# First attention: the sixth tile of each head transposed ahead of the eighth scores, the seventh right behind them

## What is computed

```python
h = _layernorm(x, axis=-1) * (1 + ca) + sa
x = x + ga * _L0_attn_ref(h, L0_attn_Wqkv, L0_attn_Wo)

# _L0_attn_ref: H = 16 heads, KV = 4 key heads, D = 128, S = 1024
xq, xk = rope(xq), rope(xk)
scores = jnp.einsum('bhsd,bhtd->bhst', q, k) * D ** (-0.5)
mask = jnp.triu(jnp.full((S, S), MASK_NEG, dtype=scores.dtype), 1)
probs = jax.nn.softmax(scores + mask[None, None], axis=-1)
att = jnp.einsum('bhst,bhtd->bshd', probs, v).reshape(B, S, H * D)
return att @ Wo
```

## Time and profile before

| | us |
|---|---|
| runs (three) | 751.27, 753.32, 753.81; median 753.32 |
| the profiled execution's own time | 751.87 |
| its span | 750.1 |
| PE busy (share of the span) | 705.2 (94%) |
| DVE busy | 550.5 (73%) |
| ACT busy | 442.1 (59%) |
| POOL busy | 386.4 (52%) |
| first attention, its 128 slots | about 38 to 434 of the span |

### The profile page before, as it was taken

How to read it: one execution, slowest core, us unless ns; L and a number is a source line. 1 busy time by engine, 2 the same in 40 slices (tenths; PEclk the granted TensorE clock), 3 DMA queues, 4 the chain that set the end, 5 groups by cost and what they waited for, 6 DMA issues and landing times. The chain is left out here.

```text
span 750.1 us, 12256 instructions
## 1 busy us (share of the span) xinstructions
PE 705.2 (94%) x4315; PEld 607.7 (81%) x4315; DVE 550.5 (73%) x1233; ACT 442.1 (59%) x921; POOL 386.4 (52%) x421
## 2 busy tenths in 40 slices
PE   8969989999999999999998889999989999899997
PEld 5858878888888888888887779998867787677787
DVE  4567686768776777687676868999788887566666
ACT  3757656666676756666665544235488767545432
POOL 3876556545863477534662322412498445116773
PEclk9999999999999999999999999999999999999999
DMA  7000001000000000004001024000100000000001
GB/s 259 15 8 8 8 22 56 9 8 15 11 20 8 15 14 10 14 8 172 20 8 50 1 59 112 1 1 1 56 2 1 1 1 1 0 3 1 1 1 58
DMA packets 19131, 19.85 MB, mean 26 GB/s; under 512 B 2174, under 2 KB 17022, under 8 KB 19070
## 3 DMA queue, kind: packets, MB, share of 16 engines
q1 hardware_dynamic: 17950, 18.40, 7.7%
q10 hardware_dynamic: 1120, 0.66, 0.3%
HBM read 18.01 MB, written 1.05 MB: 25 GB/s over the span
## 5 line engine op out<-in xcount | busy, mean ns | idle before, releaser
L909 POOL TENSOR_TENSOR at_swapped<-at_swapped,at_sin 128x512 f32<-128x512 f32 x40 | 52.1, 1303 | 130.2 <-ACT at_swapped L588 130.2
L610 ACT ACTIVATE at_probs<-at_probs,at_negmax 128x128 f32<-128x128 f32 (+7 forms) x128 | 99.6, 778 | 31.8 <-DVE at_negmax L710 29.9
L710 DVE CUSTOM_DVE_ANT_0 at_probs<-at_scores,causal 128x128 f32<-128x128 f32 (+7 forms) x128 | 96.0, 750 | 17.4 <-PE at_scores L60 16.3
L501 PE MATMUL at_turn<-ident_sb,at_probs 128*128 128x128 f32 x576 | 85.0, 274 | 11.3 <-DVE at_full_T_lo L726 9.1
L501 PEld LDWEIGHTS at_turn<-ident_sb,at_probs 128*128 128x128 f32 x576 | 66.5, 140 | 19.8 <-issue 11.4
L603 ACT ACTIVATE at_edge_T_hi<-at_turn 128x128 fp32r<-128x128 f32 (+3 forms) x128 | 55.5, 434 | 33.4 <-PE at_turn L501 33.0
L58 PE MATMUL at_scores<-at_kT_hi,room 128*128 128x512 f32 (+1 forms) x192 | 66.3, 345 | 3.4 <-DVE at_negmax L710 3.4
L603 ACT ACTIVATE at_full_T_hi<-at_turn 128x512 fp32r<-128x512 f32 x64 | 38.2, 597 | 49.8 <-PE at_turn L501 47.6
L59 PE MATMUL at_scores<-at_kT_lo,room 128*128 128x512 f32 (+1 forms) x192 | 66.5, 347 | 0.0
L60 PE MATMUL at_scores<-at_kT_hi,room 128*128 128x512 f32 (+1 forms) x192 | 66.5, 346 | 0.0
L726 DVE TENSOR_TENSOR at_edge_T_lo<-at_turn,at_edge_T_hi 128x128 fp32r<-128x128 f32 (+3 forms) x128 | 61.3, 479 | 1.3 <-ACT at_edge_T_hi L603 0.8
(11 more groups left out here) (445 smaller groups left out, 2294.9 us busy)
## 6 DMA issues: line engine op xcount, KB each, us to landing
at_wq_in<-L_attn_Wqkv SPq DMA_DIRECT2D x16, 128.0 KB, 2.2
at_wo_in<-L_attn_Wo SPq DMA_DIRECT2D x16, 128.0 KB, 2.0
staging<-L_ffn_routed_w SPq DMA_DIRECT2D x7, 256.0 KB, 4.5
wmod<-L_wmod SPq DMA_DIRECT2D x2, 768.0 KB, 4.3
at_wmod<-L_wmod SPq DMA_DIRECT2D x1, 1024.0 KB, 9.0
staging<-L_ffn_w_gate SPq DMA_DIRECT2D x1, 1024.0 KB, 6.2
staging<-L_ffn_w_up SPq DMA_DIRECT2D x1, 1024.0 KB, 8.3
staging<-L_ffn_w_down SPq DMA_DIRECT2D x1, 1024.0 KB, 10.7
```

What stands on the lines that cost most here:

```text
L501: mm = pe.transpose(p_turn[t % 2][:, b - b0, :], probs[:, s % 4, b * P:(b + 1) * P], m.ident[:, :])
L610: act.activation(row, row, ACT.Exp, scale=-1.0, bias=negmax[:, unit % 4:unit % 4 + 1], accum_out=rowsum[:, unit // NT % 2, i:i + 1])\
L710: dve.tensor_tensor_reduce(out=probs[:, s % 4, 0:width], in0=p_scores[s % 2][:, 0:width], in1=m.causal[:, S - width:], scale=-1.0, scalar= ...
L909: turning = pool.tensor_tensor(swapped[:, r % 2, :], swapped[:, r % 2, :], sin[:, cols], ALU.mult)
```

## The change

In slot 7 of every head, PE transposes tile 5 ahead of the scores of tile 7 and tile 6 right behind them. In slot 0 no tile is transposed any more. ACT writes the high half of tile 6 ahead of the exponentials of tile 7. DVE writes the low half of tile 5 ahead of the maximum of tile 7 and the low half of tile 6 behind it, both ahead of the add of the output projection. The same instructions are issued, 3349 rows of PE, 980 of DVE and 681 of ACT in both; only the order is another. GpSimd and the DMA queues keep theirs.

```diff
@@ PE, slot @@
+                    if i == NT - 1:
+                        turn(unit - 2)
                     scores(g, h, i)
                     if unit < 4:
                         value_job(4 + unit)
-                    if unit >= 2:
+                    if i == NT - 1:
+                        turn(unit - 1)
+                    elif unit >= 2 and i:
                         turn(unit - 2)
@@ PE, behind the slots @@
-                turn(KV0 * UNITS - 2)
@@ ACT, slot @@
-                    if unit >= 2:
+                    if unit >= 2 and i:
                         probs_hi(unit - 2)
+                    if i == NT - 1:
+                        probs_hi(unit - 1)
@@ ACT, behind the slots @@
-                probs_hi(KV0 * UNITS - 2)
@@ DVE, slot @@
+                    if i == NT - 1:
+                        probs_lo(unit - 2)
                     maximum(unit)
                     if i == 2 and head:
                         inverse_sums(head - 1)
-                    if unit >= 2:
+                    if i == NT - 1:
+                        probs_lo(unit - 1)
+                    elif unit >= 2 and i:
                         probs_lo(unit - 2)
@@ DVE, behind the slots @@
-                probs_lo(KV0 * UNITS - 2)
```

## The result

| | before | changed |
|---|---|---|
| median of the runs (17 each, us) | 752.78 | 754.85 |
| lowest and highest | 750.29 to 754.03 | 753.27 to 756.69 |
| ratio, 95% interval | | 1.0029 (1.0019 to 1.0040) |
| profiled execution: time, span | 751.87, 750.1 | 755.24, 753.4 |

The changed kernel takes 1.4 to 3.0 us more. The forecast was 754.6 with 1.3 us more by its sum. The time lies in the range, and in the upper half of the likeliest case's own (753.4 to 755.9). That the two times differ by 0.25 only is in part luck: the forecast started from a median of three runs, 753.32, which lies 0.54 above the one of 17, and its sum of 1.3 was 0.8 short of the 2.07 measured.

A forecast was written before the change was run, and what follows sets the result against it. TensorE is busy nearly throughout, so only its waits can give: 9.1 us in 17 places for DVE's low half. Terms 1.00 + 0.38 + 1.25 - 1.98 - 0.2 - 0.1 + 0.93 = +1.3 us give 754.6, range 750.4 to 757.0.

The forecast's parts named there:

- Direction, and no measurable gain: Whole kernel: +1.3 us by the sum, most likely no measurable change, since under 0.3% can hardly be told from none.
- estimate of 744.8: Whole kernel: counting all gaps aimed at as gain, 9.1 us less 0.55, gives 744.8; 3 in 100.
- PE takes tile 6 early, gains 0.21: Ordinary head end, tile 6's transposes: PE stalls 0.32 instead of some 0.53, gaining about 0.21 up to here.
- DVE 0.93 later, 0.69 of cover, 0.25 left: Ordinary head end: short maximum 0.93 later, ACT's slack covers 0.69, query projection copies and PE 0.24 to 0.25 later.
- Key ends lose the same, through the add of slot 5: Ends of heads 2, 5, 6, 9, 10, before a key projection: 0.25 lost each through a late add, +1.25 together.
- Third end, +0.38: Third head's end: DVE did not idle 0.14 there, so 1.07 of delay against 0.69 of cover, +0.38.
- Between groups -0.66 each: Three ends between groups: the 0.98 stall at tile 7 goes, 0.32 at tile 6 comes; -0.66 each, -1.98 together.
- First, 15th, last: Head ends: first -0.2, 15th -0.1, last +0.93 because tile 6's low half stands ahead of the second add.
- What the profile was to show: Changed profile: tile 6 wait about 0.15, none at tile 7 between groups, 0.6 or more ahead of `attend`.
- Rival 1: Ordinary and key ends: slack 0.93 or more, so nine ends gain 0.21 each; faster, 750.1; 20 in 100.
- rival 2: Slower, 756.6: between groups PE waits for ACT, price 1.98; or slack 0.15 smaller, price 1.5; 20 in 100.
- Rival 3: Whole kernel: the order hides itself, PE's waits move and no term survives; 753.3; 15 in 100.

The follow-up runs named there:

- e3: Changed kernel, but DVE writes the low half of tile 6 behind the short maximum again; 751.11 us, ratio 0.9976 to before.
- e5: Changed kernel, last end as before, tile 6's low half early on DVE only at ends 1, 4, 8, 12, 15; 747.88 us, ratio 0.9931 to before.
- e9: Changed kernel with two unused matmuls filling PE's wait in the third head, ahead of slot 5's output projection; 754.86 us, ratio 1.0028 to before.
- e2: Changed kernel with the last head's end as before; 753.45 us, ratio 1.0013 to before.
- e1: Kernel before with the change only at the ends of heads 1, 4, 8, 12 and 15; 749.42 us, ratio 0.9960 to before.
- e8: Kernel before with only tile 5 moved ahead of slot 7's scores, tile 6 left in slot 0; 756.22 us, ratio 1.0045 to before.
- e6: e5 with five DVE gate steps moved from the third head into the fourth; 747.02 us, ratio 0.9916 to before.
- e7: Kernel before with only the five DVE gate steps moved from the third head into the fourth; 750.38 us, ratio 0.9970 to before.
- e4: Changed kernel with five DVE gate steps moved from the third head into the fourth; 753.57 us, ratio 1.0007 to before.

## Why the prediction was right, and where it was short

- **Direction, and no measurable gain: right.** Closing nearly all of the 9.1 us gave no time back; the kernel is 0.29% slower, clear of noise and under the 0.3% that the prediction called hard to tell from none. The rule of the Trainium skill (Perfetto Trace Analysis, Optimization Strategy) with its estimate of 744.8 did not hold for this edit as it stood. What decided here is that the producer made earlier pushed other work of its own engine back (5.42 in place of 4.44 for the short maximum).
- **PE takes tile 6 early, gains 0.21: right.** In e3 and e5, where DVE's delay is gone, the ordinary and key ends gain 0.17 to 0.28 each, the third 0.08 and 0.10.
- **DVE 0.93 later, 0.69 of cover, 0.25 left: the mechanism right, the size 0.06 too small.** The walk let the low half of tile 6 start when DVE is done with the long maximum. DVE was done at 210.84, when it read the maximum out, and before, the next low half stood right at such a read. Now it starts at 210.90, which is 0.63 behind ACT's high half (210.27), and ACT follows the transposes (209.60) by 0.67. All 16 ends show these 0.66 to 0.67 and 0.63, and 0.05 to 0.06 of idle DVE. The walk had used 0.63 for both hand-overs and so found DVE and the chain through PE and ACT level, at 3.52 and 3.53 behind the slot's start; the chain comes last. Ten ends at about 0.07 make 0.7 of the 1.36 by which the steps exceed the forecast; the clock (below) is 0.83, and the ends between groups give 0.13 back.
- **Key ends lose the same, through the add of slot 5: right.** Ends 5 to 7 and 9 to 11 sum to 0.31 and 0.33 an end, and the waits of 0.36 to 0.41 for the add are there.
- **Third end, +0.38: the term that failed.** With its neighbour it was to cost 0.63 and cost 1.57. By e9, 0.83 of that is the clock: with the wait filled the two cost 0.76, in line with some 0.06 more an end. The walk carried DVE's delay on to a PE wait of 1.67 us that was there already, and took the work behind it at its old price: it put the clock behind the longer wait at nothing. (That DVE did not idle ahead of the long maximum there is not in rows 8, which show PE; the trace of before has it, the add at 107.64 and the maximum at 108.42, the 0.78 that an add costs.)
- **Between groups -0.66 each: right** (-0.70), and the gain is DVE's early low half (e3 against e5), whereas the text credited the early transposes and the early drain together.
- **First, 15th, last: the sizes right** within 0.12. e2 shows the last one by itself: it is worth 0.97. But the prediction put all of its +0.93 down to the low half of tile 6 ahead of the add, and e3, without that, still loses 0.77. The size was right in part by luck.
- **What the profile was to show: mostly right.** The wait ahead of `attend` was to grow to 0.6 or more and stayed at 0.20; the other 0.43 stands ahead of the transposes of tile 0'.
- **Rival 1** (slack of 0.93 or more) is refuted by `attend` at 9.78 against the bound of 9.47. The slack was 0.67, the 0.98 by which the short maximum comes later less the 0.31 of `attend`, and so not 0.15 under the 0.69 either, the other form of rival 2. **Rival 2** (between groups PE waits for ACT) did not occur: 237.47 has no bracket. **Rival 3** fell with e1 and e2, whose terms survive one by one.
- **Two slips in the numbers.** The range of 750.4 to 757.0 was to go from rival to rival, and these were priced at 750.1 and 756.6. And the chances count 3 of rival 1 both as same and as faster, and leave out 3 of rival 2. Neither touches the forecast.

## What to carry to other kernels

When work on an in-order engine is moved forward, list what it moves back, and follow the first of these that someone waits for; here a drain 0.9 us early on DVE cost the ordinary and key ends 0.3 each, and paid 0.7 at the three between groups, where DVE would have idled. A rule applied to every end of a loop hides two edits with opposite signs: split by kind of end, the same idea went from +2.1 us to -5.2, and to -6.1 with one unrelated block of DVE work moved off the longest wait. Before adding to a wait of TensorE that is already long, read the granted clock behind it, since the work that follows can cost more than the wait.

## What the runs showed of the hardware

The granted clock fell from 1.00 to 0.50 (2.4 to 1.2 GHz) shortly after PE had resumed from a wait of 2.27 us (changed kernel) or 2.24 us (e2), and was back at 1.00 some 3 us later under steady work. That the clock falls behind idle time, and comes back by work, is also what the Trainium skill says (TensorE: Matmul & The Clock Gate, Part 1). All falls in the eleven traces, those at the very start and end of the program left out:

| wait of PE, us | place | traces with it | clock fell in |
|---|---|---|---|
| 2.27, 2.24 | third head, slot 5 | changed, e2 | both |
| 1.67 to 1.72 | the same | before, e1, e3, e5, e8 | none |
| 1.88 | 15th end, tile 7 | e8 | e8 |
| 1.88 to 1.91 | behind the stage, at 546 to 556 | all eleven | before, e6, e9 |
| 1.22 to 1.25, then about 1.0 | first head, at 44 to 48 | all eleven | e7, e8 |
| others of 1.2 to 1.7 | first head to behind the stage | some in each | none |

So a single wait can bring the fall in a stage where PE is busy nearly all the time, and the same wait brings it in one execution and not in another. Behind the first four kinds the drop came 0.3 (e2), 0.6 (changed) and up to 1.4 us (e9) after PE had resumed, on matmuls that wait for nothing; in e7 and e8 it came within the second wait of the first head.

The price of one fall was 0.83 us in the third head (changed against e9) and 0.85 behind the 15th end (e8). Behind the stage, the distance from the matmul after that wait to the one after the next wait of 1.24 us was 75.57 to 75.95 us in the three traces with a fall and 75.08 to 75.14 in the eight without, so 0.4 to 0.9. In the first head (e7) it was nothing.

The spread of whole executions goes with the clock too. Of the 30 of before beside e1 to e4, the six with a mean granted clock of 0.999 took 751.24 to 751.64, the five with 0.991 took 754.06 to 754.55. That is more than the 2.07 us between the two kernels, so their difference shows only over many executions of each.
